# Fetching half of the routed rows with indirect transfers, and a third slot for the gated result

## What is computed

```python
xn = _layernorm(x)
s  = causal_attention(xn, WQ, WK, WV)            # 8 x 512 x 256

# feed-forward with 8 experts; all tokens in one flat list xf (4096 x 256)
scores  = softmax(xf @ w_gate.T)
# 2 of 4 groups are kept, then the 2 best experts of a token: topk_idx, weights
counts   = bincount(topk_idx.reshape(-1), length=8)
flat_idx = topk_idx.reshape(-1)                  # 8192 numbers between 0 and 7
routed_in  = xf[flat_idx] * weights.reshape(-1, 1)
h          = silu(grouped_mm(routed_in, w1, counts)) * grouped_mm(routed_in, w3, counts)
routed_out = grouped_mm(h, w2, counts)
shared     = silu(xf @ sw1.T) * (xf @ sw3.T) @ sw2.T
out        = shared.at[flat_idx].add(routed_out)
g = silu(out)
x = x + s * g
```

## Time and profile before

| | |
|---|---|
| median of 3 runs | 239.04 us (238.71 to 239.35) |
| the profiled execution | 240.62 us, of which the span of the trace is 238.6 us |
| PE busy | 230.6 us (97% of the span), 1533 matmuls |
| DVE, ACT, POOL busy | 186.8, 144.9 and 55.4 us |
| granted TensorE clock, mean | 0.993 of full |
| DMA | 19.45 MB, 82 GB/s over the span |

### The profile page before, as it was taken

The page is one execution under the profiler, slowest core; times in us unless marked ns, Lnnn a source line. Parts: engine busy times, 40 slices in busy tenths (PEclk is TensorE's granted clock), DMA queues, the critical chain, the costliest instruction groups (busy, mean ns, idle before and its releaser), DMA issues.

```text
span 238.6 us, 4677 instructions
## 1 busy us (share of the span) xinstructions
PE 230.6 (97%) x1533; PEld 205.8 (86%) x1533; DVE 186.8 (78%) x620; ACT 144.9 (61%) x392; POOL 55.4 (23%) x108
## 2 busy tenths in 40 slices
PE   7898999999999999999999999999999999999983
PEld 5788998998989989999899998898988889898843
DVE  3779859989899899897977985677776867869765
ACT  2444745755648457474574723779678696878722
POOL 5220631805509136073012000002020201202000
PEclk9999999999999999999999979999999999999999
DMA  5699420020200200000000000116847557393523
GB/s 156 207 326 304 157 91 1 1 87 5 88 3 0 88 3 3 0 3 0 0 3 1 0 3 0 48 26 196 142 105 197 76 145 122 103 199 57 140 74 102
DMA packets 18758, 19.45 MB, mean 82 GB/s; under 512 B 1064, under 2 KB 17712, under 8 KB 18736
## 3 DMA queue, kind: packets, MB, share of 16 engines
q1 hardware_dynamic: 15568, 16.02, 21.4%
q0 software_dynamic: 3168, 3.15, 9.1%
HBM read 14.95 MB, written 4.21 MB: 80 GB/s over the span
## 4 chain that ended last, share of the span: by engine, by line
PE 92%; DMA 2%; DVE 2%; ACT 1%; issue 1%; SPq 1%; DVEq 0%; ACTq 0%
PE bank L392 85%; PE bank L484 4%; PE bank L440 3%; DMA raw_qkv<-in_L_attn_WK 2%; DVE raw_sw L1382 1%; DVE w L1380 1%; PE bank L556 1%; PE bank L414 0%; SPq L220 0%; DVE arena L949 0%; ACT xT_hi_all L731 0%; ACT arena L731 0%; ACT probs L731 0%; ACT attn_all L731 0%; SPq L222 0%
## 5 line engine op out<-in xcount | busy, mean ns | idle before, releaser
L392 PE MATMUL bank<-xT_hi_all,arena 128*128 128x512 f32 (+3 forms) x256 | 80.7, 370 | 0.7 <-DVE arena L949 0.7
L392 PE MATMUL bank<-arena 128*128 128x256 f32 (+2 forms) x560 | 76.8, 285 | 0.3 <-ACT attn_all L731 0.3
L392 PEld LDWEIGHTS bank<-arena 128*128 128x128 f32 (+1 forms) x560 | 71.9, 186 | 5.0 <-issue 0.8
L392 PEld LDWEIGHTS bank<-xT_hi_all,arena 128*128 128x128 f32 x256 | 47.0, 189 | 8.3 <-ACT probs L761 1.4
L731 ACT ACTIVATE arena<-bank 128x512 fp32r<-128x512 f32 (+4 forms) x84 | 36.2, 452 | 24.4 <-PE bank L392 23.1
L949 DVE TENSOR_TENSOR arena<-bank,arena 128x264 fp32r<-128x264 f32 (+4 forms) x83 | 41.4, 508 | 6.9 <-ACT arena L731 6.0
L392 PE MATMUL bank<-xT_lo_all,arena 128*128 128x512 f32 (+3 forms) x128 | 45.8, 358 | 0.0
L383 POOL DMA_DIRECT2D x_ring<-in_L_attn_x x6 | 7.9, 1317 | 79.0 <-DVE x_ring L1318 79.0
L392 PEld LDWEIGHTS bank<-xT_lo_all,arena 128*128 128x128 f32 x128 | 24.2, 189 | 2.1
L731 ACT ACTIVATE attn_all<-bank,row_inv 128x256 f32<-128x256 f32 x32 | 15.2, 474 | 17.3 <-PE bank L392 15.5
L761 ACT ACTIVATE probs<-bank,neg_max 128x128 f32<-128x128 f32 (+3 forms) x32 | 17.0, 530 | 12.6 <-DVE neg_max L1008 12.5
(11 more groups left out here) (128 smaller groups left out, 381.9 us busy)
## 6 DMA issues: line engine op xcount, KB each, us to landing
x_ring<-in_L_attn_x SPq DMA_DIRECT2D x7, 512.0 KB, 3.5
x_ring<-in_L_attn_x POOLq DMA_DIRECT2D x6, 512.0 KB, 6.0
out<-x_ring SPq DMA_DIRECT2D x6, 512.0 KB, 3.3
spread<-pairs SPq DMA_DIRECT2D x14, 128.0 KB, 3.3
...
xn<-in_L_attn_x SPq DMA_DIRECT2D x1, 512.0 KB, 5.3
```

The lines of the kernel that those rows point to most:

```text
L392: return nc.tensor.matmul(dst, lhsT, rhs, start=start, stop=stop, skip_group_check=True, **kw)
```

## The change

The second half (g = 1) of the routed row tiles of stages 1 to 7 is no longer picked out on PE. The table A is also kept as plain float32 (`A_full`), turned on PE to 64 rows (`A_rows`) and stored to a table in memory. DVE makes integer pair numbers (`pair_ids`), and POOL issues for each of the four tiles one indirect transfer of 128 rows of 512 bytes from that table into `fetched`, which lies in the attention's `probs`. `silu_rows(i, 1)` reads `fetched`, not the bank, and waits for these transfers. The g = 1 one-hots and the g = 1 loads of spread pair numbers of these stages are gone. `fetch_rows(i)` overwrites `fetched`, so it waits until all `silu_rows` of stage i-1 are done. The gated result has three slots in place of two; the third is `gate`, which before only the last stage used.

```diff
+        pair_ids = sb("pair_ids", [P, NR], mybir.dt.uint32)
+        A_full = raw_sw[:, 2, 0, 0:PAIRS]
+        A_rows = raw_sw[0:PAIRS, 2, 1, 0:H]
+        fetched = probs[:, 0, :].rearrange("p (r h) -> p r h", r=RG)
+        A_dram = nc.dram_tensor("A_table", [PAIRS, H], F32).ap()
...
+        def gated_at(i):
+            return gate if i % 3 == 2 else x_ring[:, i % 3, :, :]
...
             def load_pairs(i):
-                for g in range(2):
-                    if i > 1:
-                        sp.wait_ge(s["one_hot_done"], 2 * (i - 1) + g + 1)
-                    rows = pairs_dram[i * RB + g * RG:i * RB + (g + 1) * RG, :].rearrange("r p -> (r p)")
-                    sp.dma_start(spread[:, g, :], rows.unsqueeze(0).to_broadcast([P, RG * P])).then_inc(s[f"spread{g}"], 16)
+                if i > 2:
+                    sp.wait_ge(s["one_hot_done"], i)
+                rows = pairs_dram[i * RB:i * RB + RG, :].rearrange("r p -> (r p)")
+                sp.dma_start(spread[:, i % 2, :], rows.unsqueeze(0).to_broadcast([P, RG * P])).then_inc(s[f"spread{i % 2}"], 16)
+
+            sp.wait_ge(s["a_rows_kept"], 1)
+            sp.dma_start(A_dram, A_rows).then_inc(s["a_stored"], 16)
...
             def add_x(i):
                 pool.wait_ge(s["gated"], 2 * (i + 1))
-                pool.dma_start(x_ring[:, i % 2, :, :], x_v[sequence(i), :, :, :], accum_op=ALU.add).then_inc(s[f"summed{i % 2}"], 16)
+                pool.dma_start(gated_at(i), x_v[sequence(i), :, :, :], accum_op=ALU.add).then_inc(s[f"summed{i % 3}"], 16)
+
+            def fetch_rows(i):
+                if i > 1:
+                    pool.wait_ge(s["rows_silu"], RB * i)
+                for j in range(RG):
+                    r = i * RB + RG + j
+                    pool.indirect_dma_start(fetched[:, j, :], None, A_dram,
+                                            bass.IndirectOffsetOnAxis(pair_ids[:, r:r + 1], 0)).then_inc(s["rows_in"], 16)
 
+            pool.wait_ge(s["p_turned"], T * B)
+            pool.wait_ge(s["a_stored"], 16)
+            pool.wait_ge(s["ids_ready"], 1)
+            fetch_rows(1)
             for i in range(B - 2):
+                fetch_rows(i + 2)
                 add_x(i)
...
             pe.wait_ge(s["a_split"], 2)
-            nc.tensor.transpose(x_bank[0][:, 0:P], A_T[:, :].bitcast(F32), ident[:, :]).then_inc(s["a_turned"], 1)
+            nc.tensor.transpose(x_bank[0][:, 0:P], A_T[:, :].bitcast(F32), ident[:, :])
+            nc.tensor.transpose(x_bank[0][0:PAIRS, P:2 * P], A_full, ident[:, :]).then_inc(s["a_turned"], 1)
...
                 gather(i, 0)
                 hidden(i, 1, 0, h1_bank, "h1_done")
                 shared_out(i - 1, 1)
-                gather(i, 1)
                 hidden(i, 1, 1, h3_bank, "h3_done")
                 accumulate(i - 1, 1)
...
             act.wait_ge(s["tables_summed"], 4)
+            copy(A_full, x_bank[0][:, 0:PAIRS])
             copy(A_T[:, 0:PAIRS], x_bank[0][:, 0:PAIRS]).then_inc(s["a_split"], 1)
             keep_attn(b, 3)
             act.wait_ge(s["a_turned"], 1)
+            copy(A_rows, x_bank[0][0:PAIRS, P:2 * P]).then_inc(s["a_rows_kept"], 1)
...
             def silu_rows(i, g):
                 act.wait_ge(s["route"], ROUTED)
-                act.wait_ge(s["gathered"], 2 * i + g + 1)
+                if i > 0 and g == 1:
+                    act.wait_ge(s["rows_in"], 16 * RG * i)
+                else:
+                    act.wait_ge(s["gathered"], i + 2 if i > 0 else g + 1)
...
             def silu_out(i, half):
                 act.wait_ge(s["o_done"], 2 * i + half + 1)
-                if isinstance(i, int) and i < 2:
+                if i < 2:
                     act.wait_ge(s["xn_done"], B - 1 + i)
-                else:
-                    act.wait_ge(s[f"out_stored{i % 2}"], 16 * (i // 2))
+                elif i > 2:
+                    act.wait_ge(s[f"out_stored{i % 3}"], 16 * (i // 3))
...
             for t, src in enumerate((o_bank, acc_bank, g_bank, bc_bank)):
                 act.wait_ge(s["last_tile_done"], t + 1)
+                act.wait_ge(s["out_stored2"], 16 * 2)
...
             pair_one_hots(0, 0)
             h_mult(0, 0)
+            nc.vector.tensor_scalar(pair_ids[:, :], pair_rows[:, :], 8.0, None, ALU.add).then_inc(s["ids_ready"], 1)
...
                 gate_attn(i - 1, 0).then_inc(s["gated"], 1)
-                one_hot(i, 1)
                 h_mult(i, 0)
```

39 lines of the change are left out of this document (20 added, 19 removed).

## The result

The changed kernel took **240.60 us** (median of 20 runs, 239.64 to 243.22) beside 239.13 us of the kernel before (20 runs, 238.71 to 242.71): a ratio of **1.0074, 95% interval 1.0053 to 1.0095**. It is slower by 0.7%, where the prediction said 236.9 us.

The account below looks back on a forecast made before the run. PE was taken to bound the stages. Removed gathers -2.94 us, an added transpose +0.11 and stage 7's late rows +0.7 gave -2.1: 239.04 to 236.9 us; forecast's own range 236.2 to 238.3, whole range 236.0 to 241.5.

Parts of the forecast that it names:

- A gather: On PE in the stages: each gather costs 0.42 us, so removing seven brings 2.94 us.
- The middle stage without a wait: Stages 2 to 6: 10.29 us falls to 9.87, PE busy throughout, rows there 1.3 us early.
- The fetch pitch: On POOL: each of a stage's four fetch issues takes 1.28 us, as add_x's issue does; ends 0.32 and 1.5.
- X: Fetch loop: time from a stage's first fetch issue to its last landing, 7.3 us, ends 2.5 and 9.0.
- The two rivals that ended best and in the middle: No stall in stage 7: 236.2 us, chance 0.18. DVE held up by POOL's fetches: 238.9 us, chance 0.09.
- the 0.2 us of X: POOL's fetches beside DVE's one-hot of the next stage: 0.2 us added to X for their overlap.
- the term L = 2.0 us: Fetch loop: the landing behind a stage's last fetch issue takes 2.0 us, between 1.2 and 3.0.
- the 8.6 at which the loop is the bound: Middle stages: the loop of fetch and silu becomes the bound at X = 8.6 us.
- the rival that it gave 0.19: Fetch loop becomes the bound: beyond X = 8.6 each us is paid in six stages, 240.5 at 9.0; chance 0.19.
- about 0.1 for semaphores: Fetch loop, stage to stage: about 0.1 us beside 1.14 for four silus and X; 1.24 beside X in all.
- Stage 7: silu_rows(7, 1) stands earlier on ACT, so its rows come 0.7 us late; 2.2 us gained, not 2.94.
- The cover of the third slot: Gated result: slot free after 14.6 us, wanted at about 26 with three, about 16 with two; third slot covers add_x's delay.

Follow-up runs that it names:

- e10: e5 with two slots for the gated result in place of three: 236.07 us, ratio 0.985.
- e5: Changed kernel with two buffers for the fetched rows, a stage's fetches starting behind silu_rows(i-1, 0), half a stage sooner: 236.29 us, ratio 0.989.
- e1: The changed kernel once more, no edit, a second profile: 241.43 us (one run).
- e12: The changed kernel again, no edit, a third profile: 241.22 us (one run).
- e11: Changed kernel with silu_out(6, 0) ahead of silu_rows(7, 1) on ACT: ratio 1.002 (0.998 to 1.006).
- e13: Changed kernel plus four 64 KB stores before the stages, into the part of the output that store(0) overwrites later: 240.19 us, ratio 1.003.
- e6: Changed kernel without add_x for the six batches; the store waits for the gate instead: 240.22 us, ratio 1.005.
- e14: Changed kernel with store(0) held back until stage 3's rows have landed, and each spread load issued one stage sooner: 239.74 us, ratio 1.002.
- e3: Changed kernel with the fetch of stage 1 only, its rows reused in stages 2 to 7: 236.29 us, ratio 0.9885.
- e4: Changed kernel with two buffers for the fetched rows, fetches starting behind silu_rows of two stages before: 238.60 us, ratio 0.998.
- e8: Kernel with all gathers on PE as before, three slots, and 28 fetches beside them into rows nobody reads: 239.46 us beside 239.12, ratio 1.0007.

## Why the prediction was wrong

**What was right.** A gather is 0.42 us: seven should bring 2.94, and from the first group of 20 to `routed_out` e10 needs 68.53 us against 71.44 before, 2.91 less. The middle stage without a wait is 9.85 (9.87 forecast). The fetch pitch is 1.34 us, 1.04 and 0.30 (1.28 forecast), and X by the packets is 7.1 to 7.3 in five of the changed kernel's six later groups (7.3 forecast). The chain from `silu_rows(7, 1)` to `accumulate(7, 1)` takes 225.66 - 221.50 = 4.16 (4.1 forecast). The two rivals that ended best and in the middle are out: no gain beyond the forecast's, and DVE's instructions of `h_mult` to `h_low` have the durations of the earlier trace rows; the one-hot takes 480 to 483 ns in the changed kernel against the 616 that the 0.2 us of X came from the earlier trace rows, and 526 in the median of e5. By the Trainium skill (SBUF — State Buffer, "Who interferes with whom") a DVE instruction in a two-port mode and one of GpSimd would hold each other up for the whole instruction; on DVE the rows show 0.04 us in e5 and none in the changed kernel. On POOL the second fetch of a group, beside `h_low` and the one-hot, took 1.31 and 1.38 us in two groups and 1.04 to 1.07 in four, where the same instructions lie beside it; its cause wasn't tested.

**What failed** is the term L = 2.0 us, taken as one value for all stages: "16 KB land 1.7 us after issue ... I take 2.0", with 3.0 as its end. With nothing beside it a fetch does land in 1.9, but in stage 3 it took 4.1 to 4.8 us in every profile of the changed kernel, beyond the upper end. By the prediction's own sum that puts X at 9.3 to 9.9, over the 8.6 at which the loop is the bound: the rival that it gave 0.19. Only it isn't paid in six stages, as that rival had it, but in one or two. (As an estimate by the Trainium skill's page DMA: Bandwidth & Descriptors, "Anatomy of one DMA", 64 KB from POOL would take 2.15 us from issue, and X be 6.0; from the start of the last issue to the last packet the runs show 2.8 at best.)

The second term that failed is the "about 0.1 for semaphores" of the same sum. Between the end of a group's silus and POOL's first issue pass 0.27 us, and between the last packet and the silu that waits for it 0.34 to 0.65 us, for which nothing was put. With the silu's own 1.27 that is 1.9 to 2.2 us beside X, not 1.24. So the bound was too high as well: in the stages without a late signal that did wait, X less the wait is 7.7 to 8.0 (e1, e12, e11, e13, and stage 2 of e6 and e14), where 8.6 was forecast. The middle stages had 0.6 to 0.9 us of slack over the usual 7.1 and not 1.3, and any L over 2.7 to 2.8 costs time (in the same stages, L less the wait).

That the measured 240.6 lies near this rival's 240.5 at X = 9.0 is luck: the rival loses in six stages, the kernel loses in three ways, of which the landing is one.

The account of the changed kernel against e10, which has no waits, in the profiles from the first group of 20 to `routed_out`: 72.67 - 68.53 = 4.14 us. Of it:
- stage 3, the slow landing: 11.05 - 9.84 = 1.2
- stages 4 to 6, 0.37 each: 1.1, which no term of the prediction had: the gather's signal reaching ACT 0.7 us late (`silu_rows(i, 0)` waits 0.98 us, 0.31 in e10), which makes `h_low` late for PE
- stage 7: 10.82 - 9.01 = 1.8, against 0.7 forecast

2.91 won and 4.14 lost is 1.2 us slower, as the full-clock runs are (1.1). In the profile another 1.7 went to the half clock.

**Stage 7** was right in mechanism and mis-sized. From the start of `silu_rows(6, 1)` to that of `silu_rows(7, 1)` were forecast 219.9 - 211.4 = 8.5 us and measured 9.3, and 10.0 in e1 with its L of 2.8, against the 7.9 that ACT needs otherwise. The silu from SBUF is 1.27 against 1.14, 0.27 us pass from silu to first issue where 0.1 was put, X is 7.09 for 7.3, and the greatest piece is the 0.65 from the last packet to the silu, which the sum left out: 1.27 + 0.27 + 7.09 + 0.65 = 9.28. With no slack at that place each of these is paid in full.

**The late signal** was in no one's list. It was there in 7 of the 9 profiles in which the fetches start behind `silu_rows(i-1, 1)` and the rows are used, in one to five stages of each, and never in e3, nor in e5 and e10, whose last fetch of a stage ends 3 us before the gather does. e4 has it once, in stage 1, and e8 once, in stage 2. The place of POOL's issues against the gather doesn't make it by itself: in e1 and e13, which have none, and in most stages of e8 the last issue ends 0.1 to 0.2 us ahead of the gather's end, as in the late stages. What holds the signal was not found; it isn't `add_x` (e6).

**The cover of the third slot** was reasoned wrongly too: by its own numbers the slot is free at 14.6 us and with two slots wanted at 16, which is still in time. e10 shows it for the earlier start; the changed kernel itself was not run with two slots.

**Left open:** why the landing is slow beside the first output store and not beside the later ones at the same distance. Twelve profiles with the first store beside a stage's fetches have it (3.3 to 4.8 us; e6 in stage 2), stage 3 of e14 without it has not; e13 speaks against the first write to that place, and e6 shows that it doesn't need `add_x`. But in all twelve a spread load lies beside the same fetches, and such a load without a store goes with 3.1 us in e14 and with 1.9 in e8, both in stage 2. So which of the two transfers does it is open as well, and the 3.3 of e6 may be the spread load's. Stage 1 shows that no store is needed: loads beside it do the same. Of the later stores, those issued some 4 us ahead of the last fetch's end go with landings of 1.9 to 2.8 us (3.0 and 3.9 once each), those issued 1.2 to 1.6 us ahead with 4.1 to 4.7 (e5, stage 4; e10, stages 4 to 6).
